# A rotation's eight matrix squarings: by four pairs at once, and half of the pairs summed on TensorE and taken out by ScalarE

## The chip, the cores and the metric

The kernel runs on one core of a Trainium2 chip. The time is device microseconds of one execution. Engines are called PE (TensorE), DVE (VectorE), ACT (ScalarE), POOL (GpSimd) and SP (the engine that issues DMAs here). The kernel before takes 2093.96 us, the median of three runs from 2091.3 to 2096.46 us.

## The reference, cut to what matters

Sixteen samples x[s] of 256 x 288 are first rotated, and then go through three layers of attention and a feed-forward part. The change is in the rotation alone:

```
v = silu(cond) @ W.T + b              # 2016 numbers per sample
A = skew-symmetric 64 x 64 matrix of v
R = expm(A)                           # one rotation per sample
Q = orthonormal basis of P (288 x 64) # by elimination
x = x + x Q (R - I) Q^T               # in effect: x is rotated in the space of P
# then three layers: attention, gelu/feed-forward, modulated by cond
```

## The kernel before

`prepare` does the rotation; it ends about 170 us into the span, and the three layers take the rest. It does two things at the same time.

**The elimination.** DVE orthogonalises P column by column, in nine phases k = 0 to 8 of eight steps i each. A step is a chain of seven small dependent instructions (sign, turn, update of the tile, reciprocal, factors, next column, outer product: L969 to L1015) of 0.15 to 0.23 us. Between two phases PE, DVE and ACT hand over to each other (`change_phase` on PE, `norms`, `whole_t_out`, `both_out` on ACT): DVE writes `whole` (L1022), PE transposes it (L574, chain_a and chain_b), DVE writes `spread`, ACT writes the norms and copies `whole_t` (L462, L463, L467), and PE multiplies by `whole_t` (L593, L595), which starts the next phase.

**The exponential.** A is scaled by 2^-8, its exponential E (less the identity) comes from a power series, and is squared eight times: with E for exp - I, one squaring is 2E + E·E. Since A is skew, the tile `ef` (here with the trace's name skew_ef) holds for each of eight pairs of samples E and its transpose (m = 0 and 1), 128 columns of a pair; the two samples of a pair lie on the lower and upper 64 partitions. A squaring in one round of all samples is 4 fills f: `square(f)` on PE makes the products of two pairs (8 matmuls, 16 records in the trace, because a 4-byte matmul is recorded twice) into half of bank ps_a or ps_b in turn, and `squared(f)` on DVE (L922) computes 2·ef + bank over 256 columns and writes ef. There are 32 fills. The table `places` puts each `squared` behind a step of the elimination on DVE: eight in phase 5, nine each in 6 and 7, six in 8. The table `SQUARES` spreads the matmuls in the same way over PE's program.

**Other work in these phases.** For two samples per phase PE transposes x (`transposed`, L629), ACT copies the transposed pieces out (`transposed_out`, L431, L432), and PE multiplies them (`in_space`, L637). In phases 6 and 8 PE also computes the modulation (`modulation_rows`, L673, L677; ACT copies them, L444, L445; `modulation_columns` on PE, L685; `mods_out` on ACT, L453). In phases 6, 7 and 8 ACT rounds weights of the first layer (`high_weights`, L418), in program order ahead of the norms of the phase.

Every engine runs its program in the order written in its function of `prepare`; nothing is scheduled by a planner. After phase 8, DVE makes `diag`, `inv_beta` and `c_mat`, then `low_weights(0)` (L1090), and then copies `c_t` (L1095) from the matmul at L737; the rotations, the differences and the first layer's q and k follow from c_t.

Of the kernel before, what the change touches and what calls it, by code (L numbers as in the profile page):

```python
# [8 lines left out]
ALU = mybir.AluOpType  # L9
# [50 lines left out]
def prepare(nc, dram, keep, early):  # L60
# [10 lines left out]
    with ExitStack() as ctx:  # L71
# [30 lines left out]
        even = sb("even", [P, NPAIR, R])  # L102
        mod_rows = sb("mod_rows", [P, L, ROW_COLS])
# [73 lines left out]
        s_exp = sem("s_exp")  # L177
        s_square_ps = sem("s_square_ps")
# [48 lines left out]
        FILLS = 4 * SQUARINGS  # L227
        GROUPS = ((0, 5), (5, 10), (10, B))

        SQUARES = {5: range(0, 8), 6: range(8, 17), 7: range(17, 26), 8: range(26, FILLS)}  # L230

# [22 lines left out]

        def pairs_of(f):
            return slice(2 * (f % 4), 2 * (f % 4) + 2)
# [113 lines left out]
        def _(act):  # L370
# [21 lines left out]
            A(gram_norm[TOP, 0:1], unit[TOP, 0:1], ACT.Sqrt)  # L392
            for half in range(2):
                A(twin[:, half, :], unit[TOP, TOP_COLS], ACT.Copy).then_inc(s_twin, 1)
# [43 lines left out]
            def powers_out(n):  # L438
                act.wait_ge(s_product, n + 1)
                A(powers[:, :, n, :], (ps_a, ps_b)[n][:, :].rearrange("p (n c) -> p n c", c=R), ACT.Copy).then_inc(s_power, 1)  # L440

# [41 lines left out]
            for k in range(PHASES):  # L483
# [11 lines left out]
                if k == POWERS_AT:  # L495
                    powers_out(0)
                    powers_out(1)
                for s in INPUTS.get(k, ()):
                    transposed_out(s)
                    if s % 2:  # L500
                        in_space_out(s // 2)
# [3 lines left out]
                if k in (6, LAST):  # L505
                    mod_rows_out(k // LAST)
                    mods_out(k // LAST)
# [50 lines left out]
        def _(pe):  # L558
# [97 lines left out]
            def square(f):  # L656
                bank = (ps_a, ps_b)[f % 2]
                pe.wait_ge(s_exp, 2 + max(f - 1, 0))
                pairs = range(pairs_of(f).start, pairs_of(f).stop)
                for i, n in enumerate(pairs):  # L660
# [31 lines left out]
            for k in range(PHASES):  # L692
# [24 lines left out]
                for i, f in enumerate(SQUARES.get(k, ())):  # L717
                    square(f)
                    if i == 1:
                        transposed(INPUTS[k][0])  # L720
                    if i == 3:
                        transposed(INPUTS[k][1])
                    if i == 5:
                        in_space(INPUTS[k][0] // 2)
                    if k == 6 and i == 6:
                        modulation_rows(0)
                    if k == 6 and i == 8:
                        modulation_columns(0)
                if k == LAST:
                    modulation_rows(1)  # L730
                    modulation_columns(1)
# [3 lines left out]
            pe.wait_ge(s_twin, 2)  # L735
# [5 lines left out]
            pe.wait_ge(s_exp, 2 + FILLS)  # L741
# [94 lines left out]
        def _(dve):  # L836
# [82 lines left out]
            def squared(f):  # L919
                dve.wait_ge(s_square_ps, f + 1)  # L920
                here = ef[:, pairs_of(f), :, :].rearrange("p n m c -> p (n m c)")
                V.scalar_tensor_tensor(out=here, in0=here, scalar=2.0, in1=(ps_a, ps_b)[f % 2][:, 0:256],  # L922
                                       op0=ALU.mult, op1=ALU.add).then_inc(s_exp, 1)
# [20 lines left out]
            DONE = len(places)  # L944
# [1546 lines left out]
```

## Time and profile before

| what | value |
|---|---|
| median of three runs | 2093.96 us |
| the profiled execution's own time | 2095.36 us |
| its span | 2093.7 us |
| PE busy, its weight loads busy | 94%, 84% |
| DVE, ACT, POOL busy | 58%, 54%, 48% |
| mean granted TensorE clock | 0.967 |
| first squaring's matmuls | at 73.24 us |
| c_t (behind the last phase) | at 129.99 us |

The shares are means over the span, and nearly all of the span is the layers. The change lies between 73 and 130 us, so only the timeline of that stretch tells what it does. PE there is shown twice in a timeline: PEld are weight loads, and PE are matmuls, whose ends are modelled. The clock column PEclk is 1.00 for 2.4 GHz and 0.50 for 1.2 GHz.

### The profile page before, as it was taken

The page shows a single profiled execution, that of the slowest core. Times are in us where ns is not written, and L with a number is a line of the kernel's source. Part 1 is how long each engine was busy: PE and PEld are TensorE (multiplying, and loading weights), DVE is VectorE, ACT ScalarE, POOL GpSimd, SP SyncE. Part 2 cuts the span into 40 slices and gives each one's busy share as a digit, 9 for nine tenths or more (in the row PEclk, how much of TensorE's full clock was granted, in tenths as well). Part 3 has the DMA queues.
Part 4 walks back from the last instruction along what each step waited for, and adds up shares of the span by engine and source line. Part 5 has one row for each costly group of instructions (what it writes and reads, how often), then busy time and mean ns, then how long its engine had stood idle before and what let it go on. Part 6 is the DMA issues. An engine that isn't in the chain of part 4 may idle for free. (4 is left out here: it accounts for less than half of the span.)

```text
span 2093.7 us, 49820 instructions
## 1 busy us (share of the span) xinstructions
PE 1977.5 (94%) x16599; PEld 1757.2 (84%) x16599; DVE 1205.1 (58%) x2656; ACT 1120.6 (54%) x1928; POOL 1006.7 (48%) x1037
## 2 busy tenths in 40 slices
PE   5886799999999999899999999998999999999996
PEld 3554589899999998789899998997889998999986
DVE  7874556556465575556565465575565465554641
ACT  5322464655656645555655646555555646556552
POOL 1002455455554554655454454555655554555534
PEclk9787899999999999999999999999999999999998
DMA  7514433333323333433333323333433323333320
GB/s 204 134 61 120 145 101 80 103 90 92 99 80 106 97 84 102 152 100 90 94 87 101 99 80 103 91 92 99 135 86 99 99 79 105 92 91 96 84 81 26
DMA packets 138467, 207.01 MB, mean 99 GB/s; under 512 B 35720, under 2 KB 95718, under 8 KB 137318
## 3 DMA queue, kind: packets, MB, share of 16 engines
q1 hardware_dynamic: 110338, 168.31, 29.2%
q10 hardware_dynamic: 25332, 29.74, 5.2%
q0 software_dynamic: 2704, 7.77, 1.4%
q8 instruction: 53, 0.87, 0.2%
q14 instruction: 40, 0.33, 0.1%
HBM read 99.18 MB, written 20.82 MB: 57 GB/s over the span
## 5 line engine op out<-in xcount | busy, mean ns | idle before, releaser
L2255 DVE TENSOR_REDUCE maxima<-scores 128x4 f32<-128x1024 f32 x384 | 460.9, 1223 | 180.4 <-PE scores L2011 173.4
L1618 POOL TENSOR_TENSOR hidden<-g_full,hidden 128x512 fp32r<-128x512 f32 (+1 forms) x240 | 280.5, 1176 | 356.6 <-ACT hidden L1852 355.4
L1809 ACT ACTIVATE probs<-scores 128x1024 f32<-128x1024 f32 x384 | 383.2, 1027 | 98.7 <-PE pv_ps L2048 58.8
L2073 PE MATMUL mlp_ps<-h_mlp,w_up 128*128 128x256 f32 (+1 forms) x3024 | 404.6, 286 | 5.0 <-POOL h_mlp L1618 3.4
L2073 PEld LDWEIGHTS mlp_ps<-h_mlp,w_up 128*128 128x128 f32 (+1 forms) x3024 | 378.6, 190 | 35.4 <-issue 19.4
L1936 PE MATMUL mlp_ps<-w_down,hidden 128*128 128x288 f32 x2592 | 390.8, 296 | 0.0
L1936 PEld LDWEIGHTS mlp_ps<-w_down,hidden 128*128 128x128 f32 x2592 | 370.0, 189 | 18.6
L2011 PE MATMUL scores<-k_stack,q_stack 108*128 108x512 f32 x768 | 241.9, 407 | 8.9 <-DMA k_stack<-qk 6.8
L2034 PE MATMUL scores<-q_stack,k_stack 110*128 110x256 f32 x1536 | 247.0, 293 | 3.4 <-ACT probs L1809 2.2
L2034 PEld LDWEIGHTS scores<-q_stack,k_stack 110*128 110x128 f32 x1536 | 209.3, 192 | 33.0 <-issue 18.9
L1799 ACT ACTIVATE neg_max<-att_ps 16x256 fp32r<-16x256 f32 x48 | 17.9, 374 | 380.9 <-PE att_ps L2021 380.9
L1686 POOL TENSOR_TENSOR o_full<-o_full,inv_sum 128x512 f32<-128x512 f32 x96 | 139.7, 1475 | 156.1 <-DVE o_att L2267 156.1
L2260 DVE RECIPROCAL inv_few<-sums 128x32 f32<-128x32 f32 x48 | 16.9, 353 | 317.5 <-DMA sums<-sum_scratch 317.5
L1851 ACT ACTIVATE g_full<-mlp_ps 128x512 f32<-128x512 f32 (+1 forms) x240 | 133.4, 556 | 122.5 <-PE mlp_ps L2073 61.3
L1618 POOL TENSOR_TENSOR h_mlp<-h_full,h_mlp 128x512 fp32r<-128x512 f32 x48 | 72.5, 1510 | 260.0 <-DVE h_mlp L2221 259.8
L2048 PE MATMUL pv_ps<-probs,v_sb 128*32 128x256 f32 x3072 | 190.0, 388 | 0.6 <-ACT probs L1809 0.6
L1936 PE MATMUL mlp_ps<-w_out,o_att 128*128 128x288 f32 x1152 | 173.3, 301 | 5.1 <-issue 4.1
L1936 PEld LDWEIGHTS mlp_ps<-w_out,o_att 128*128 128x128 f32 x1152 | 159.7, 192 | 6.9 <-issue 4.5
L2011 PEld LDWEIGHTS scores<-k_stack,q_stack 108*128 108x128 f32 x768 | 129.2, 194 | 21.6 <-DVE maxima L2255 8.8
L2048 PEld LDWEIGHTS pv_ps<-probs,v_sb 128*32 128x32 f32 x3072 | 91.0, 111 | 65.9 <-issue 4.1
L1985 PE MATMUL att_ps<-h_att,w_in 128*126 128x256 f32 (+3 forms) x987 | 134.3, 283 | 1.6 <-DVE qk L2231 0.9
L1852 ACT ACTIVATE hidden<-mlp_ps 128x512 fp32r<-128x512 f32 (+1 forms) x240 | 132.0, 550 | 0.0
(263 smaller groups left out, 2843.4 us busy)
## 6 DMA issues: line engine op xcount, KB each, us to landing
q_stack<-qk SPq DMA_DIRECT2D x144, 180.0 KB
k_stack<-qk SPq DMA_DIRECT2D x282, 90.0 KB
inv_sum<-inv_scratch ACTq DMA_DIRECT2D x192, 128.0 KB, 2.7
k_stack<-qk SPq DMA_DIRECT2D x282, 54.0 KB
x_mid<-out_x SPq DMA_DIRECT2D x48, 288.0 KB, 4.2
out_x<-x_out SPq DMA_DIRECT2D x48, 288.0 KB, 3.1
x_in<-out_x SPq DMA_DIRECT2D x46, 288.0 KB, 3.9
q_stack<-qk SPq DMA_DIRECT2D x144, 72.0 KB
```

The source lines that it names most:

```text
L1618: tt(out, full, high.bitcast(F32), ALU.subtract).then_inc(signal, 1)
L1686: tt(o_full[:, half, :], o_full[:, half, :], inv_sum[:, half, :], ALU.mult).then_inc(s_o_norm, 1)
L1809: evict(probs[:, u % 4, :, :, :], scores[u % 2][:, :, :, :], ACT.Exp, scale=SCALE)\
L1851: evict(g_full[:, n % 2, 0:width], bank[:, 0:width], ACT.Gelu_apprx_tanh).then_inc(s_gelu, 1)
L1852: evict(hidden[0][:, tiles, :].rearrange("p a t -> p (a t)"), bank[:, 0:width], ACT.Gelu_apprx_tanh)\
L1936: last = mm(out, a(left), c(weights[w]), start=start and n == 0, stop=stop and n == total - 1)
L1985: last = mm(qk_bank[n][0:cols.stop - cols.start, (m % 2) * T:(m % 2 + 1) * T], w[:, cols], h, start=count == 0, stop=count == 6)
L2011: last = mm(scores[u % 2][:, qt, :, :], q_stack[r, u, qt * P:(qt + 1) * P], k_stack[r, u, :, :], start=True, stop=True)
L2034: last = mm(scores[u % 2][:, par, kt, :], k_stack[r, u, par, kt * P:(kt + 1) * P], q_stack[r, u, :], start=True, stop=True)
L2048: last = mm(pv_ps[32 * i:32 * i + 32, (g % 2) * T:(g % 2 + 1) * T], v_sb[:, kt, 4 * g + i, :], probs[:, u % 4, i % 2, kt, :], start=kt == ...
L2073: last = mm(up_bank[n % 2][:, (m % 2) * T:(m % 2 + 1) * T], w[:, m * P:(m + 1) * P], h, start=count == 0, stop=count == 6)
L2255: nc.vector.tensor_reduce(out=maxima[:, :, :, u], in_=scores[u % 2][:, :, :, :], axis=AX.X, op=ALU.max).then_inc(s_max, 1)
```

## The change

Round r of the squarings now works on four pairs at once. Pairs 0 to 3 stay with DVE: PE writes all of their products into the whole of ps_a (16 matmuls), and DVE adds 2·ef over 512 columns. For pairs 4 to 7, PE also multiplies ef by a new constant `twice` (two times the identity) and accumulates this and the product in ps_b (32 matmuls); ACT then copies the 512 columns out to ef. Each of phases 5 to 8 holds two rounds: DVE's part stands behind steps 2 and 6 (5 in the last phase), PE's at the start of the phase and behind `in_space`, and ACT's ahead of `transposed_out` and ahead of `mods_out` and `high_weights`. `modulation_rows` now stands ahead of the second round on PE, `modulation_columns` behind it.

```
-        FILLS = 4 * SQUARINGS
-        SQUARES = {5: range(0, 8), 6: range(8, 17), 7: range(17, 26), 8: range(26, FILLS)}
+        SQUARES = {5: (0, 1), 6: (2, 3), 7: (4, 5), 8: (6, 7)}
...
+            for h, cols in ((TOP, TOP_COLS), (GRAM, GRAM_COLS)):
+                A(twice[h, :], unit[h, cols], ACT.Copy, scale=2.0).then_inc(s_twin, 1)
...
+            def squared(r):                                   # on ACT
+                act.wait_ge(s_square_ps, 2 * r + 2)
+                A(ef[:, 4:NPAIR, :, :].rearrange("p n m c -> p (n m c)"), ps_b[:, :], ACT.Copy).then_inc(s_exp_others, 1)
...
+                if k in SQUARES:                              # ACT, ahead of transposed_out
+                    squared(SQUARES[k][0])
...
+                if k in SQUARES:                              # ACT, behind mod_rows_out
+                    squared(SQUARES[k][1])
+                if k in (6, LAST):
                     mods_out(k // LAST)
                 if k in (6, 7, 8):
                     high_weights(k - 6)
...
-            def square(f):
-                bank = (ps_a, ps_b)[f % 2]
-                pe.wait_ge(s_exp, 2 + max(f - 1, 0))
+            def square(r):
+                pe.wait_ge(s_exp, 2 + r)
+                for n in range(4):
                     for m in range(2):
-                        at = (2 * i + m) * R
-                        last = halves(bank[:, at:at + R], ef[:, n, 1 - m, :], ef[:, n, m, :])
+                        at = (2 * n + m) * R
+                        last = halves(ps_a[:, at:at + R], ef[:, n, 1 - m, :], ef[:, n, m, :])
+                last.then_inc(s_square_ps, 1)
+
+            def square_others(r):
+                if r == 0:
+                    pe.wait_ge(s_twin, 2)
+                pe.wait_ge(s_exp_others, r)
+                for n in range(4):
+                    for m in range(2):
+                        at = (2 * n + m) * R
+                        for first in (True, False):
+                            for h in (TOP, GRAM):
+                                last = mm(ps_b[h, at:at + R], twice[h, :] if first else ef[h, 4 + n, 1 - m, :], ef[h, 4 + n, m, :],
+                                          start=first, stop=not first, tile_position=(h.start, h.start))
                 last.then_inc(s_square_ps, 1)
...
+                if k in SQUARES:                              # PE
+                    square(SQUARES[k][0])
+                    square_others(SQUARES[k][0])
+                    for n in INPUTS[k]:
+                        transposed(n)
+                    in_space(INPUTS[k][0] // 2)
+                    if k in (6, LAST):
+                        modulation_rows(k // LAST)
+                    square(SQUARES[k][1])
+                    square_others(SQUARES[k][1])
+                    if k in (6, LAST):
+                        modulation_columns(k // LAST)
...
-            def squared(f):
-                dve.wait_ge(s_square_ps, f + 1)
-                here = ef[:, pairs_of(f), :, :].rearrange("p n m c -> p (n m c)")
+            def squared(r):                                   # on DVE
+                dve.wait_ge(s_square_ps, 2 * r + 1)
+                here = ef[:, 0:4, :, :].rearrange("p n m c -> p (n m c)")
...
-            places = [(5, i) for i in (*range(1, 7), GAP_A, GAP_B)]
-            places += [(k, i) for k in (6, 7) for i in (*range(7), GAP_A, GAP_B)]
-            places += [(8, i) for i in range(6)]
+            places = [(k, i) for k in (5, 6, 7, 8) for i in (2, 6 if k < LAST else 5)]
```

PE in phase 6 before, from in_space (xt_ps) over modulation_rows (ada_ps from w_ada_0) to the first transpose of the change of phase (chain_a); ps_a and ps_b from skew_ef are the squarings:

```order
L637 MATMUL xt_ps<-x_t,p_nat 64x256 x6
L569 MATMUL ps_a<-skew_ef 64x64 x8
L673 MATMUL ada_ps<-w_ada,silu_c 16x352 x4
L677 MATMUL ada_ps<-w_ada,silu_c 16x144 x4
...
L569 MATMUL ps_b<-skew_ef 64x64 x8
L569 MATMUL ps_a<-skew_ef 64x64 x8
L685 MATMUL ada_ps<-ident,mod_rows 128x128 x2
L685 MATMUL ada_ps<-ident,mod_rows 96x128
L574 MATMUL chain_a<-ident,whole 64x64 x2
```

The same place of the changed kernel:

```order
L647 MATMUL xt_ps<-x_t,p_nat 64x256 x6
L696 MATMUL ada_ps<-w_ada_0,silu_c 16x352 x4
L700 MATMUL ada_ps<-w_ada_0,silu_c 16x144 x4
...
L579 MATMUL ps_a<-skew_ef 64x64 x16
L685 MATMUL ps_b<-skew_ef,twice 64x64 x2
L685 MATMUL ps_b<-skew_ef 64x64 x2
...
L708 MATMUL ada_ps<-ident,mod_rows 128x128 x2
L708 MATMUL ada_ps<-ident,mod_rows 96x128
L584 MATMUL chain_a<-ident,whole 64x64 x2
```

Between modulation_rows and modulation_columns there were 16 matmuls in two fills, and there are now 48 in one round (the last two rows on ps_b alternate, two matmuls each, eight times).

ACT in phase 7 before, from in_space's copy (w_rot_x) over the weights' rounding (w_in0) to the norms and whole_t:

```order
L436 ACTIVATE w_rot_x<-xt_ps 128x256
L418 ACTIVATE w_in0<-staging 128x5x36 x2
L418 ACTIVATE w_in0<-staging 128x2x36
L418 ACTIVATE w_in0<-staging 128x3x36
L418 ACTIVATE w_in0<-staging 128x2x18
L418 ACTIVATE w_in0<-staging 128x288
L462 ACTIVATE gram_norm<-turn 64x8
L463 ACTIVATE norm<-turn 64x8
L467 ACTIVATE whole_t<-chain_b 128x72
```

And in the changed kernel:

```order
L436 ACTIVATE w_rot_x<-xt_ps 128x256
L445 ACTIVATE skew_ef<-ps_b 128x512
L418 ACTIVATE w_in0<-staging 128x5x36 x2
L418 ACTIVATE w_in0<-staging 128x2x36
L418 ACTIVATE w_in0<-staging 128x3x36
L418 ACTIVATE w_in0<-staging 128x2x18
L418 ACTIVATE w_in0<-staging 128x288
L467 ACTIVATE gram_norm<-turn 64x8
L468 ACTIVATE norm<-turn 64x8
L472 ACTIVATE whole_t<-chain_b 128x72
```

The copy of the second round (skew_ef from ps_b) now stands ahead of the rounding and of the norms.

## Rows read from the trace of the kernel before

**Rows 1.** Windows; columns: stretch, length, busy of PE, PEld, DVE, ACT, POOL, clock, DMA, GB/s.

```profile
58.50:79.00 20.50, 18.15 (x150) 12.58 (x146) 16.90 (x92) 6.58 (x23) 0.17 (x1) 0.50 0.92 208
102.90:106.30 3.40, 3.35 (x41) 3.19 (x42) 3.05 (x17) 0.94 (x6) 0.00 (x0) 0.50 1.01 224
```

**Rows 2.** Timeline; columns: start, length, engine, line, operation, [idle before]. DVE's fills of 256 and 512 columns.

```profile
65.51 0.69 DVE L910 SCALAR_TENSOR_TENSOR odd<-ada_ps,a_pos 128x512 f32<-128x512 f32 x1
...
76.23 0.41 DVE L922 SCALAR_TENSOR_TENSOR skew_ef<-skew_ef,ps_a 128x256 f32<-128x256 f32 x1
76.56 0.15 DVE L969 TENSOR_SCALAR sign<-current 128x1 f32<-128x1 f32 x1
...
78.06 0.15 DVE L969 TENSOR_SCALAR sign<-current 128x1 f32<-128x1 f32 x1
```

**Rows 3.** Timeline: bursts of 64x64 matmuls at the low and the high clock.

```profile
73.24 0.98 PEld L569 LDWEIGHTS ps_a<-skew_ef 64*64 64x64 f32 x14
...
74.31 0.98 PEld L569 LDWEIGHTS ps_b<-skew_ef 64*64 64x64 f32 x14
...
131.00 1.01 PEld L569 LDWEIGHTS ps_a<-c_twice,skew_ef 64*64 64x64 f32 x32 [0.38 <-DVE c_twice L1097]
...
132.20 0.69 DVE L1102 COPY w_rot_x<-ps_a 128x512 f32<-128x512 f32 x1
```

**Rows 4.** Timeline, phase 6: PE and ACT in turn on the transposed input.

```profile
87.52 0.86 PE L629 MATMUL xt_ps<-ident,w_rot_x 128*96 128x128 f32 x6
...
88.42 0.59 ACT L431 ACTIVATE x_t<-xt_ps 96x512 f32<-96x512 f32 x1 [0.48 <-PE xt_ps L629]
...
88.91 0.37 ACT L432 ACTIVATE x_t<-xt_ps 96x256 f32<-96x256 f32 x1
...
90.98 0.24 PEld L629 LDWEIGHTS xt_ps<-ident,w_rot_x 128*96 128x96 f32 x2
...
92.00 0.37 ACT L432 ACTIVATE x_t<-xt_ps 96x256 f32<-96x256 f32 x1
...
93.61 1.52 PE L637 MATMUL xt_ps<-x_t,p_nat 96*64 96x256 f32 x12
...
95.05 0.54 PEld L569 LDWEIGHTS ps_a<-skew_ef 64*64 64x64 f32 x16 [0.39 <-issue]
```

**Rows 5.** Timeline: the end of phase 6, and the first squaring of phase 7.

```profile
95.66 0.13 PEld L673 LDWEIGHTS ada_ps<-w_ada,silu_c 96*16 96x16 f32 x8
...
98.30 0.54 PEld L569 LDWEIGHTS ps_b<-skew_ef 64*64 64x64 f32 x16 [0.24 <-issue]
...
99.38 0.29 PEld L685 LDWEIGHTS ada_ps<-ident,mod_rows 128*128 128x128 f32 x3
...
100.91 1.41 ACT L418 ACTIVATE w_in<-staging 128x180 fp32r<-128x180 f32 x6
102.34 0.21 ACT L462 ACTIVATE gram_norm<-turn 64x8 f32<-64x8 f32 x1
...
102.95 0.18 PEld L593 LDWEIGHTS chain_b<-both,whole_t 64*64 64x64 f32 x1 [2.14 <-ACT whole_t L467]
...
103.12 0.98 PEld L569 LDWEIGHTS ps_b<-skew_ef 64*64 64x64 f32 x14
```

**Rows 6.** Timeline: the first squarings of phases 6 and 8.

```profile
86.33 0.59 PEld L569 LDWEIGHTS ps_a<-skew_ef 64*64 64x64 f32 x15
...
116.38 0.89 PEld L569 LDWEIGHTS ps_a<-skew_ef 64*64 64x64 f32 x15
```

**Rows 7.** Timeline: behind the last step of phase 8.

```profile
127.56 0.15 DVE L969 TENSOR_SCALAR sign<-current 64x1 f32<-64x1 f32 x1
...
128.41 1.39 DVE L1090 TENSOR_TENSOR w_in<-staging,w_in 128x180 fp32r<-128x180 f32 x6
...
129.99 0.28 DVE L1095 COPY c_t<-chain_a 64x128 f32<-64x128 f32 x1 [0.19 <-PE chain_a L737]
```

**Rows 8.** Timeline: SP issues the first layer's q.

```profile
166.61 14.47 SPq L1368 DMA_DIRECT2D q_stack<-qk  x12
```

More of the change, by code:

```diff
@@ L102, in prepare @@
         even = sb("even", [P, NPAIR, R])
+        twice = sb("twice", [P, R])
         mod_rows = sb("mod_rows", [P, L, ROW_COLS])
@@ L177, in prepare @@
         s_exp = sem("s_exp")
+        s_exp_others = sem("s_exp_others")
         s_square_ps = sem("s_square_ps")
@@ L253, in x_banks @@
             return (ada_ps if s % 2 else xt_ps)[:, s % 2, :], xt_ps[:, 1, 0:T]
-        def pairs_of(f):
-            return slice(2 * (f % 4), 2 * (f % 4) + 2)
         def halves_of(k):
@@ L654, in high_powers @@
                         last.then_inc(s_product, 1)
-            def square(f):
-                bank = (ps_a, ps_b)[f % 2]
-                pe.wait_ge(s_exp, 2 + max(f - 1, 0))
-                pairs = range(pairs_of(f).start, pairs_of(f).stop)
-                for i, n in enumerate(pairs):
-                    for m in range(2):
-                        at = (2 * i + m) * R
-                        last = halves(bank[:, at:at + R], ef[:, n, 1 - m, :], ef[:, n, m, :])
+            def square(r):
+                pe.wait_ge(s_exp, 2 + r)
+                for n in range(4):
+                    for m in range(2):
+                        at = (2 * n + m) * R
[12 more added lines that the diff above has]
+                                          start=first, stop=not first, tile_position=(h.start, h.start))
                 last.then_inc(s_square_ps, 1)
@@ L716, in _ @@
                             in_space(s // 2)
[L717 to L731, printed above, removed]
+                if k in SQUARES:
[10 more added lines that the diff above has]
+                        modulation_columns(k // LAST)
                 if k < LAST:
                     change_phase(k)
-            pe.wait_ge(s_twin, 2)
+            pe.wait_ge(s_twin, 4)
             pe.wait_ge(s_c_mat, 1)
@@ L740, in _ @@
             pe.wait_ge(s_basis, 16)
-            pe.wait_ge(s_exp, 2 + FILLS)
+            pe.wait_ge(s_exp, 2 + SQUARINGS)
+            pe.wait_ge(s_exp_others, SQUARINGS)
             mm(ps_b[:, 0:C], c_t[:, :, :], p_t[:, :], start=True, stop=True).then_inc(s_u_ps, 1)
@@ L917, in exponential @@
                                        op0=ALU.mult, op1=(ALU.add, ALU.subtract)[m]).then_inc(s_exp, 1)
-            def squared(f):
-                dve.wait_ge(s_square_ps, f + 1)
-                here = ef[:, pairs_of(f), :, :].rearrange("p n m c -> p (n m c)")
-                V.scalar_tensor_tensor(out=here, in0=here, scalar=2.0, in1=(ps_a, ps_b)[f % 2][:, 0:256],
-                                       op0=ALU.mult, op1=ALU.add).then_inc(s_exp, 1)
+            def squared(r):
+                dve.wait_ge(s_square_ps, 2 * r + 1)
+                here = ef[:, 0:4, :, :].rearrange("p n m c -> p (n m c)")
+                V.scalar_tensor_tensor(out=here, in0=here, scalar=2.0, in1=ps_a[:, :], op0=ALU.mult, op1=ALU.add).then_inc(s_exp, 1)
             def inverse_norms():
@@ L940, in _ @@
             between.update({(8, 0): (inverse_norms,), (8, 1): (inverse_norms_diagonal,)})
-            places = [(5, i) for i in (*range(1, 7), GAP_A, GAP_B)]
-            places += [(k, i) for k in (6, 7) for i in (*range(7), GAP_A, GAP_B)]
-            places += [(8, i) for i in range(6)]
-            DONE = len(places)
+            places = [(k, i) for k in (5, 6, 7, 8) for i in (2, 6 if k < LAST else 5)]
             def fill(k, i):
```

## The prediction

> **What bounds the kernel now.** I read the page's busy shares first: PE leads with 94%, but that is the layers. The change lies between 73 and 130 us, so I went on to the windows and then the timeline of that stretch, engine by engine. The reader is to see two things there. In phases 5, 7 and most of 8, DVE's chain of elimination steps is the pace: its instructions follow each other without a gap, and a fill lies in it [rows 2]. At the ends of phases 6 and 8 it is not DVE: the first matmuls of phase 7 wait 2.14 us for ACT's whole_t, which stands behind the rounding of weights [rows 5], and in phase 8 c_t waits at the end for PE [rows 7]. What the change takes from DVE it gives to PE and ACT, so I work out each phase anew as a chain over all three and compare it with the phase's length before. The phases begin, by the first squaring's weight load, at 73.24, 86.33, 103.12 and 116.38 us, and c_t comes at 129.99 [rows 3, 5 to 7]: lengths 13.09, 16.79, 13.26 and 13.61 us.
>
> **What DVE is spared.** A fill of 256 columns lasts 0.41 us, but the next sign starts 0.33 behind its start; a step with one takes 78.06 - 76.56 = 1.50, so about 1.17 without. 512 columns with one operand in PSUM last 0.69 [rows 2], 0.28 more, so 0.61 in the chain. Removed: 32 x 0.33 = 10.6 us. Added: 8 x 0.61 = 4.9. If DVE alone were the pace, that would be 5.7 us less.
>
> **What PE gets.** 32 fills of 8 matmuls were 256; now 8 rounds of 16 + 32 are 384. In the trace's records (two per matmul) a round is 96. At 2.4 GHz 32 records start within 1.01 us and DVE can read the result 1.20 after the first [rows 3], so a round takes 3 x 1.01 = 3.03 us with the gaps between its parts, and DVE's part is there at 1.20. At 1.2 GHz two bursts of 16 matmuls together, 32 records, take 74.31 + 0.98 - 73.24 = 2.05, so a round 6.15. Accumulating pairs of this kind are not in the trace; I take them at the price of the plain ones. Lower bound: 16 records start within 0.54 us [rows 4], 0.027 each with the last one's own 0.13 taken off; upper bound: 15 within 0.59 right after a change of phase [rows 6], 0.033 each. With two rounds of 96 in a phase that is from -0.4 to +0.5 us per phase against the 3.03. ACT's copy of 512 columns: 0.59, the next instruction 0.49 behind its start [rows 4]; between 0.49 and DVE's 0.69, I take 0.49.
>
> **The chain of a phase.** PE's program is now: round, transposed (first sample), transposed (second), in_space, in phases 6 and 8 modulation_rows, second round, in phases 6 and 8 modulation_columns, change of phase. Before, the DVE chain hid the whole exchange with ACT between the fills; now it stands in one row with both rounds. From rows 4: the transposes start and ACT is done with the first sample 88.91 + 0.37 - 87.52 = 1.76 us later; the last transposes of the second start then, and ACT is done 92.37 - 90.98 = 1.39 later; in_space takes 95.05 - 93.61 = 1.44 until PE goes on. With 0.05 for each hand-over that is 4.70 us. A clean round ahead of it (3.03) puts the second round at 7.75, DVE's second fill at 8.95. Eliminating alone, DVE would want it at about 0.3 + 1.3 + 5 x 1.17 + 0.61 + 1.1 = 9.1, so it hardly waits there in phases without modulation, at the high clock.
>
> Phase 5. The clock is at 1.2 GHz until 79 us [rows 1], so the first round ends at about 79.15, not 76.3. Then 4.70: second round at 83.85; its 96 records end at 86.9; ACT's copy starts at 87.1 and passes ACT on at 87.6. Behind it stand the norms and whole_t: from L462's start to L593's 0.61, and to the first squaring 0.17 more [rows 5]. Phase 6 starts at 88.35 and not 86.33: +2.0 us. The new ACT copy is the instruction that delays the norms, and PE waits for them.
>
> Phase 6. Round 3.03, exchange 4.70, modulation_rows 98.30 - 95.66 = 2.64 [rows 5], second round at 10.4, its end at 13.4. modulation_columns at 13.45; from there to the rounding of weights 100.91 - 99.38 = 1.53, the rounding 1.43, norms to the next phase 0.78: 17.2 against 16.79, +0.4. DVE waits here for its second fill until 11.6 (it would be ready at 9.1), but then runs 0.61 + 1.0 to `whole` at 13.2, so it isn't what ends last.
>
> Phase 7. Before, the clock was at 1.2 GHz from 102.90 to 106.30 [rows 1], right behind the 2 us that PE sat idle for ACT. That wait stays, so I expect the low stretch again, now over a round of 96 records and not two of 16: 3.4 us at half speed are 53 records, the other 43 take 1.36, so the round takes 4.75. Exchange: second round at 9.45, end at 12.5. ACT's copy 0.15 + 0.49, and only then the rounding of weights, which before had only in_space's copy ahead of it: 1.43, and 0.78. Phase length 15.3 against 13.26: +2.05. At the high clock throughout it would be 13.6: +0.35.
>
> Phase 8. Round, exchange and modulation_rows as in phase 6: second round at 10.4, DVE's fill at 11.6. DVE wants it at about 8.6, and three more dependent pieces stand behind it: 0.61, one step of 1.1, 127.56 to 128.41 = 0.85 to low_weights, and 1.39 for that ahead of c_t [rows 7]. c_t at 15.55 against 13.61: +1.95. Before this phase PE now idles for ACT as well; with a low clock over its round it is +1.7 more. I take the middle, +2.8.
>
> Sum: 2.0 + 0.4 + 2.05 + 2.8 = 7.3 us. Behind c_t everything up to the first layer follows from it: rotations, differences, q and k, and then the q that SP sends from 166.61 on [rows 8]. I count the delay as passed on in full. The two small ACT instructions that make `twice` (0.2 us each) stand near 7 us, ahead of constants that nobody waits for yet: nothing. The profiled execution had 2095.36 us, 1.4 above the median; applied to the median of 2093.96 the sum gives 2101.3 us.
>
> By a page of the Trainium skill ("TensorE: Matmul & The Clock Gate", "Part 1: The HAM clock gate") TensorE is throttled by default and its own activity releases the clock. By that rule the change, which makes PE busier in just these phases, would speak for itself: see the first rival. The trace agrees in that the clock fell behind the idle stretch of phase 6 [rows 1, 5].
> The page "PSUM — Partial Sum Buffer", "Engine vs sequencer instructions", says in the Trainium skill that ScalarE's queue is strict first in, first out. It speaks against the change: the rounding and the norms cannot overtake the new copy. The row in which L593 waits 2.14 us for whole_t agrees [rows 5].
>
> **The rivals.**
> *The busier PE keeps its clock.* In phases 7 and 8 the rounds run at 2.4 GHz: 2.0 + 0.4 + 0.35 + 1.95 = 4.7 us, 2098.7. For it: PE has half again as many squaring matmuls. Against it: PE still idles about 2 us at the ends of 6 and 7 behind ACT, and that is what preceded the low stretch before.
> *DVE is the pace and all else is hidden.* Then the change gives the 5.7 us, 2088.3 us, just inside 0.3%. It decides from the point where the second round is ready before DVE asks, at 9.1 us into the phase, and where ACT's copy ends before the norms. For it: DVE's gapless chain. Against it: modulation_rows alone puts the second round of phases 6 and 8 behind DVE, and ACT's copy comes 3.0 us behind the second round's start, when DVE has nearly finished the phase.
> *It gets worse than that.* More of the exchange falls into low-clock stretches, since PE now works in one burst and then idles through the exchange (about 1.3 us of 4.7), and the accumulating pairs cost the upper bound: 7.3 + one stretch of 1.7 + 4 x 0.5 + the rest of phase 8's 0.8 = 11.8, 2105.8 us.
> *The delay is absorbed* by SP's and the DMA queues' 14 us behind 166.61 [rows 8], if these wait for bandwidth that was used by something not delayed: 0 to 3 us, 2095.5.
>
> **How the numbers follow.** 0.3% is 6.3 us, about what a measurement of this kernel can tell from no change. The forecast has 0.55 (its own range 4.7 to 9.7 us, about 2098.7 to 2103.7), the kept clock 0.2, DVE as the pace 0.07, worse 0.12, absorbed 0.06. Slower by over 0.3%: three quarters of the forecast and all of the worse case and a bit, 0.55. Faster: half of DVE's rival and less, 0.03. Within: 0.42. Range: 2095.5 to 2106.
>
> **What would show it.** In the profile after: PE's first squaring of phase 6 at 88.3 and not 86.3; ACT's copy of 512 columns starting after 87 us, with the norms right behind; DVE idle for 2 to 3 us ahead of its second fill in phases 6 and 8, and not in 7; the weights' rounding of phase 7 behind the second copy; c_t near 137 us. The clock column at the starts of phases 7 and 8 tells the forecast from the first rival. It is wrong if c_t comes ahead of 130 us, if DVE has no idle time in phase 8, or if a round of 96 records takes well under 3 us.

## The result, and the profile after

The changed kernel takes 2100.61 us (median of 8 runs, 2094.05 to 2104.41) against 2093.78 us for the kernel before (8 runs, 2089.16 to 2098.02). The ratio is 1.0033, with a 95% interval from 1.0017 to 1.0050: 6.8 us slower. The profiled execution has 2103.66 us and a span of 2101.7 us. All ratios here are of executions in one state; a single one of the twelve of run r3, at 2126.03 us and a mean granted clock of 0.898, is left aside as slow.

The phases can be followed by PE's first load behind whole_t (L593 before, L603 after), which starts each phase; lines from here on are those of the kernel named. c_t is DVE's copy that ends the stretch. The forecast's lengths count from the first squaring's load, 0.1 us behind that.

| | phase 5 | phase 6 | phase 7 | phase 8 to c_t | c_t behind the start of phase 5 |
|---|---|---|---|---|---|
| before | 13.15 | 16.73 | 13.31 | 13.73 | 56.9 |
| changed | 14.20 | 20.20 | 15.13 | 15.51 | 65.0 |
| forecast | 15.1 | 17.2 | 15.3 | 16.4 | 64.0 |

c_t comes at 137.98 us, 7.99 later than before [rows 7]. Behind it the delay stays: SP issues the first q at 175.70, 9.1 later than in [rows 8], the first load of x_mid is issued 8.7 us later and the last 7.8 (210.9 and 2036.3 against 202.2 and 2028.5).

First PE's weight loads in phases 5 and 6 of the changed kernel, from the timeline (start, length, engine, line, operation, [idle before and its releaser]):

```profile
73.11 1.83 PEld L579 LDWEIGHTS ps_a<-skew_ef 64*64 64x64 f32 x30
...
78.19 0.61 PEld L639 LDWEIGHTS xt_ps<-ident,w_rot_x 128*96 128x96 f32 x6
...
82.83 1.01 PEld L579 LDWEIGHTS ps_a<-skew_ef 64*64 64x64 f32 x32 [0.39 <-issue]
...
85.51 0.20 PEld L685 LDWEIGHTS ps_b<-skew_ef 64*64 64x64 f32 x4
...
87.14 0.13 PEld L603 LDWEIGHTS chain_b<-both,whole_t 64*64 64x64 f32 x1 [0.30 <-ACT whole_t L472]
...
95.20 0.15 PEld L696 LDWEIGHTS ada_ps<-w_ada,silu_c 96*16 96x16 f32 x8 [0.64 <-issue]
...
100.29 1.52 PEld L579 LDWEIGHTS ps_a<-skew_ef 64*64 64x64 f32 x32 [0.46 <-issue]
...
107.34 0.13 PEld L603 LDWEIGHTS chain_b<-both,whole_t 64*64 64x64 f32 x1 [2.17 <-ACT whole_t L472]
```

Compare with [rows 3 to 5]. The exchange of the transposed input is 82.83 - 78.19 = 4.64 us, as worked out from the rows of before (4.70). The second round of phase 5 takes 85.51 + 0.20 - 82.83 = 2.88 us at the high clock (3.03 had been counted). modulation_rows, though, take 100.29 - 95.20 = 5.1 us, where [rows 5] have 2.64.

ACT in the same kernel: its second copies (L445), what stands behind them, and the norms (L467):

```profile
85.90 0.60 ACT L445 ACTIVATE skew_ef<-ps_b 128x512 f32<-128x512 f32 x1 [2.56 <-PE ps_b L685]
86.52 0.21 ACT L467 ACTIVATE gram_norm<-turn 64x8 f32<-64x8 f32 x1
...
103.86 0.60 ACT L445 ACTIVATE skew_ef<-ps_b 128x512 f32<-128x512 f32 x1 [2.79 <-PE ps_b L685]
...
105.30 1.41 ACT L418 ACTIVATE w_in<-staging 128x180 fp32r<-128x180 f32 x6
106.73 0.21 ACT L467 ACTIVATE gram_norm<-turn 64x8 f32<-64x8 f32 x1
...
119.97 0.60 ACT L445 ACTIVATE skew_ef<-ps_b 128x512 f32<-128x512 f32 x1 [2.56 <-PE ps_b L685]
120.46 1.37 ACT L418 ACTIVATE w_in<-staging 128x180 fp32r<-128x180 f32 x6
121.86 0.21 ACT L467 ACTIVATE gram_norm<-turn 64x8 f32<-64x8 f32 x1
```

In phases 5 and 7 ACT's copy ends right ahead of the norms or of the rounding that they stand behind; in phase 6 the modulation's columns (`mods_out`, 104.36 to 105.44) come between the copy and the rounding. In phase 7 the rounding (120.46) was in ACT's idle time before and is in the row now. A copy passes ACT on after 0.49 to 0.62 us.

DVE's second fill in phases 5 to 8, and c_t:

```profile
84.03 0.69 DVE L944 SCALAR_TENSOR_TENSOR skew_ef<-skew_ef,ps_a 128x512 f32<-128x512 f32 x1 [1.45 <-PE ps_a L579]
...
102.00 0.69 DVE L944 SCALAR_TENSOR_TENSOR skew_ef<-skew_ef,ps_a 128x512 f32<-128x512 f32 x1 [5.46 <-PE ps_a L579]
...
118.11 0.69 DVE L944 SCALAR_TENSOR_TENSOR skew_ef<-skew_ef,ps_a 128x512 f32<-128x512 f32 x1 [1.37 <-PE ps_a L579]
...
134.11 0.69 DVE L944 SCALAR_TENSOR_TENSOR skew_ef<-skew_ef,ps_a 128x512 f32<-128x512 f32 x1 [3.05 <-PE ps_a L579]
...
137.98 0.28 DVE L1113 COPY c_t<-chain_a 64x128 f32<-64x128 f32 x1
```

DVE is no longer the pace in any of the four phases; ahead of its four second fills it waits 11.3 us in all for PE's products. The wait in phase 6 is twice what was forecast (2 to 3 us), and the part beyond the forecast goes with the clock: in the second profile below, where the clock is up, it is 2.23 us. One window of that stretch (busy us of PE, PEld, DVE, ACT, POOL; then clock, DMA, GB/s), first in this profile, and then in a second profile of the same kernel (r1 below). What made the clock fall in one and not in the other stays open.

```profile
94.80:101.30 6.50, 6.50 (x70) 2.86 (x68) 1.59 (x10) 1.03 (x3) 0.00 (x0) 0.50 0.00 0
```

```profile
94.80:101.30 6.50, 6.29 (x157) 4.78 (x145) 2.88 (x15) 1.95 (x11) 0.00 (x0) 1.00 0.59 132
```

### The profile page after: what moved, and what is told of

Same layout as the page of the kernel before. It is cut to its first block and busy times, and to the rows that moved or that the text cites. A ratio compares the mean times of both kernels' runs of the same rounds, so it can differ in the third digit from the quotient of the medians.

```text
span 2101.7 us, 50320 instructions
## 1 busy us (share of the span) xinstructions
PE 1976.9 (94%) x16855; PEld 1762.0 (84%) x16855; DVE 1199.0 (57%) x2632; ACT 1126.6 (54%) x1938; POOL 1007.0 (48%) x1037
```

## The experiments

All kernels build on the changed one unless said otherwise. The two columns of the table that decide are the ratio to the kernel before, of many runs, and c_t behind the start of phase 5 in one profile each. The clock falls at other places in each execution, so a phase in which it was low for over 1 us is marked *.

| | ratio, 95% interval | phase 5 | 6 | 7 | 8 | c_t behind start |
|---|---|---|---|---|---|---|
| before | 1 | 13.15 | 16.73 | 13.31* | 13.73* | 56.9 |
| changed | 1.0033 (1.0017 to 1.0050) | 14.20 | 20.20* | 15.13* | 15.51 | 65.0 |
| r1, changed again | one run | 13.32 | 16.98 | 14.91* | 15.50 | 60.7 |
| r2, changed again | one run | 14.25 | 20.20* | 14.98* | 16.90* | 66.3 |
| e1 rows last | 1.0005 (0.9992 to 1.0019) | 14.05 | 17.61 | 14.89* | 14.98 | 61.5 |
| e2 weights first | 1.0017 (1.0003 to 1.0031) | 14.62* | 15.70 | 16.53* | 15.51 | 62.4 |
| e3 all on DVE | 0.9987 (0.9974 to 0.9999) | 13.08 | 16.64* | 12.76* | 16.09* | 58.6 |
| e4 no doubled | 0.9987 (0.9974 to 1.0001) | 12.42 | 15.11 | 12.87* | 16.08* | 56.5 |
| e5 interleaved | 0.9959 (0.9947 to 0.9971) | 12.43 | 13.76 | 14.84* | 13.95* | 55.0 |
| r3, e5 again | 0.9965 (0.9951 to 0.9980) | 12.48 | 13.76 | 14.51* | 13.30* | 54.1 |
| e6 before, weights first | 0.9994 (0.9982 to 1.0006) | 13.14 | 15.48 | 13.31 | 14.17* | 56.1 |
| e7 filler | 1.0037 (1.0022 to 1.0052) | 14.82 | 17.51 | 16.73* | 17.61* | 66.7 |
| e8 interleaved, all on DVE | 0.9966 (0.9952 to 0.9980) | 13.09 | 12.89 | 12.69 | 13.72* | 52.4 |
| e9 before reordered | 0.9984 (0.9971 to 0.9997) | 13.15 | 14.04 | 13.08 | 13.43* | 53.7 |

(The start of phase 5 is at the low clock in all of them; the * of e2 there is a second low stretch.)

### The same kernel twice more: r1, r2

> The changed kernel once more, for another profile. If the low clock over modulation_rows in phase 6 (94.8 to 101.3 us in the first profile) belongs to this order, it shows again at that place and phase 6 takes about 20 us; if it depends on how the execution happens to lie against the clock, it is elsewhere or gone and phase 6 takes 17 to 17.5 us.

> The same again: a third profile of the changed kernel, with the same two readings as the second.

No edit. 2099.98 and 2100.77 us. The low clock over modulation_rows shows in two of three profiles of the changed kernel. Phase 6 is 20.20, 16.98 and 20.20 us: with the clock up it is the forecast's 17.2. These rows are from r1, and stand against those of the first profile above:

```profile
94.34 0.13 PEld L696 LDWEIGHTS ada_ps<-w_ada,silu_c 96*16 96x16 f32 x8 [0.39 <-issue]
...
96.97 1.01 PEld L579 LDWEIGHTS ps_a<-skew_ef 64*64 64x64 f32 x32 [0.24 <-issue]
...
99.92 0.29 PEld L708 LDWEIGHTS ada_ps<-ident,mod_rows 128*128 128x128 f32 x3
...
103.52 0.18 PEld L603 LDWEIGHTS chain_b<-both,whole_t 64*64 64x64 f32 x1 [2.17 <-ACT whole_t L472]
```

modulation_rows take 2.63 us here in place of 5.1, and the 3.2 us between the two lengths of phase 6 go with the low stretch. c_t is 3.8 us later than before in r1 and 8.1 in the first profile. So about half of what one profile says of c_t can be the clock's luck, and single profiles are to be compared phase by phase, with the clock beside them.

### What the added matmuls cost: e4

This kernel leaves out the summand 2E for pairs 4 to 7, and so doesn't compute the rotation; only its time is used.

```
-                        for first in (True, False):
-                            for h in (TOP, GRAM):
-                                last = mm(ps_b[h, at:at + R], twice[h, :] if first else ef[h, 4 + n, 1 - m, :], ef[h, 4 + n, m, :],
-                                          start=first, stop=not first, tile_position=(h.start, h.start))
+                        last = halves(ps_b[:, at:at + R], ef[:, 4 + n, 1 - m, :], ef[:, 4 + n, m, :])
```

> The changed kernel without the matmuls of the doubled matrix: for pairs 4 to 7 the sum 2E is left out and only E*E is made and copied, so PE does 64 and not 96 records per round. Theory (every PE microsecond of a round is in the row but for the last): 7 rounds shorter by 0.93 us each, one or two of them at half clock by 1.9, so c_t 7 to 9 us earlier, at 129 to 131, near the kernel before. Rival (order is all: where a round stands matters and not how long it is): c_t less than 3 us earlier.

c_t 8.5 us earlier than in the changed kernel's first profile (56.5 against 65.0), 2090.86 us, ratio 0.9987. Without the clock's part: phase 6 is 15.11 against 16.98 in r1, and phase 7, with a low stretch in both, 12.87 against 14.91. Two rounds per phase shorter by 32 records each should give 2 x 0.93 = 1.9, and give 1.87 and 2.04. In phases 6 and 7 PE's time in both rounds is in the row, microsecond for microsecond. For phase 8 the fair partner is r2, with a low stretch at the start of both: 16.08 against 16.90, 0.8 us. Only the first of its two rounds lies ahead of DVE's second fill there, and c_t comes 3.87 us behind that fill in e4, r2 and the changed kernel alike.

### What ACT's order costs: e2

```
+                if k in (6, 7, 8):
+                    high_weights(k - 6)
                 if k in (6, LAST):
                     mod_rows_out(k // LAST)
                 if k in SQUARES:
                     squared(SQUARES[k][1])
                 if k in (6, LAST):
                     mods_out(k // LAST)
-                if k in (6, 7, 8):
-                    high_weights(k - 6)
```

> The changed kernel, with ACT's rounding of weights (high_weights, 1.4 us) ahead of mod_rows_out and of the second copy, in time in which ACT waits. Theory (the norms stand in a row behind the second copy and the rounding): phases 6 and 7 are 1.4 us shorter each, c_t at about 135.1, the time 2.9 us below the changed kernel. Rival (the granted clock alone explains the added time): c_t stays at 138 but for what the clock does.

Phase 6: 15.70 against 16.98 in r1, 1.3 us shorter, close to the 1.4 expected. In phase 7 the norms do follow the copy at once:

```profile
115.84 1.38 ACT L418 ACTIVATE w_in<-staging 128x180 fp32r<-128x180 f32 x6
118.51 0.60 ACT L445 ACTIVATE skew_ef<-ps_b 128x512 f32<-128x512 f32 x1 [1.29 <-PE ps_b L685]
119.13 0.21 ACT L467 ACTIVATE gram_norm<-turn 64x8 f32<-64x8 f32 x1
```

but the phase was no shorter, since something else came in: 3.26 us in which PE stood still within a round, for nothing that the profile shows, and a low clock behind it. Less these 3.26 us it would have 13.3 (14.91 in r1), which fits the 1.4 us but doesn't show them. By the two ratios the time is 3.3 us below the changed kernel's, where 2.9 were expected, but the intervals overlap (1.0003 to 1.0031 against 1.0017 to 1.0050), so the gain in time isn't shown; what is shown is phase 6.

```profile
108.64 0.13 PEld L685 LDWEIGHTS ps_b<-skew_ef,twice 64*64 64x64 f32 x1 [3.26 <-issue]
```

### Whether DVE's idle time is the cost: e1

```
                     in_space(INPUTS[k][0] // 2)
-                    if k in (6, LAST):
-                        modulation_rows(k // LAST)
                     square(SQUARES[k][1])
                     square_others(SQUARES[k][1])
                     if k in (6, LAST):
+                        modulation_rows(k // LAST)
                         modulation_columns(k // LAST)
```

> The changed kernel, with modulation_rows moved behind the second round on PE (and ACT's second copy ahead of mod_rows_out). DVE's idle time ahead of its second fill in phases 6 and 8 (5.5 and 3.1 us in the changed kernel) should mostly go. Theory (PE's program in a row, with ACT's copies and norms behind it, is the length of a phase; DVE's idle time lies beside it): PE's sum of work per phase is unchanged and modulation_columns now wait 0.6 us for ACT's rows, so c_t comes within about 1 us of the changed kernel's 137.98 us, and the time is the changed kernel's, about 2100 to 2102. Rival (DVE's idle time is the cost): c_t 5 to 8 us earlier, 130 to 133, and the time near that of the kernel before.

The clean comparison is phase 8, at the high clock here and in the changed kernel: DVE's wait for the second fill goes from 3.05 to 0.41 us, but the phase from 15.51 to 14.98 only, because c_t now waits for PE:

```profile
127.79 0.69 DVE L942 SCALAR_TENSOR_TENSOR skew_ef<-skew_ef,ps_a 128x512 f32<-128x512 f32 x1 [0.41 <-PE ps_a L578]
...
133.77 0.28 DVE L1111 COPY c_t<-chain_a 64x128 f32<-64x128 f32 x1 [2.03 <-PE chain_a L755]
```

Phase 6 is 17.61 against r1's 16.98, 0.6 longer, as worked out. So DVE's idle time lies beside PE's row, and taking it away gives 0.5 us or costs 0.6. The time, however, was 2094.43 us, ratio 1.0005, where no change against the changed kernel's 1.0033 was expected. The expectation missed here. c_t in the one profile (61.5) is 3.5 us below the first profile of the changed kernel and 0.8 above r1's, so it isn't the place. The traces show where the time went: behind c_t, where the instructions are the same. Each line of this table gives the time from c_t to SP's first load of x_mid, the mean granted clock in it, and SP's loads of x_mid from the first to the last, over the layers:

| | c_t to first x_mid | clock | first to last x_mid |
|---|---|---|---|
| before | 72.2 | 0.71 | 1826.3 |
| changed, r1, r2 | 72.9, 71.9, 71.8 | 0.69, 0.71, 0.71 | 1825.4, 1826.9, 1823.2 |
| e1 | 67.7 | 0.78 | 1823.4 |
| e2, e4 | 69.7, 69.0 | 0.75, 0.76 | 1822.4, 1823.7 |
| e3, e8 | 70.4, 71.5 | 0.74, 0.71 | 1825.9, 1824.3 |
| e5, r3 | 67.8, 69.9 | 0.80, 0.76 | 1823.7, 1821.7 |
| e6, e9 | 67.8, 66.3 | 0.78, 0.79 | 1832.2, 1826.3 |
| e7 | 71.7 | 0.74 | 1820.6 |

On the whole the stretch behind c_t is the shorter, the less of it lies at the low clock, and e1's is 4 to 5 us shorter than the changed kernel's. More than one execution says so: the mean granted clock of e1's ten runs is 0.973, and that of the changed kernel's eight 0.969 (0.969 and 0.967 in r1 and r2). Why this order meets fewer low stretches stays open. A ratio of these kernels thus holds two things, c_t and what the clock does behind it.

### The clock, filled up: e7

```
+            def filler(r, count):
+                pe.wait_ge(s_exp_others, r + 1)
+                for n in range(count):
+                    at = n % 8 * R
+                    halves(ps_b[:, at:at + R], ef[:, 4, 0, :], ef[:, 4, 1, :])
...
                     if c == 2:
+                        if s in (9, 11, 13, 15):
+                            filler(s - 9, 6)
                         pe.wait_ge(s_xt, 2 * s)
...
+                    filler(SQUARES[k][0], 10)
                     in_space(INPUTS[k][0] // 2)
```

The second piece stands in transposed: the filler writes ps_b ahead of each sample's third column block, and again ahead of in_space.

> The changed kernel, with matmuls whose result is overwritten (into ps_b) where PE waits for ACT between the transposes and ahead of in_space, 12 and 20 matmuls a phase. Theory of the clock (the low stretch over modulation_rows in phase 6 follows from PE's idle time in the exchange): the clock column stays at 1.00 from about 80 us to the end of phase 6, modulation_rows take 2.6 us and not 5.1, and phase 6 is 16.8 to 17.5 us and not 20.2; c_t at about 135. Rival (the low stretch has another cause, or the fillers cost what they bring): phase 6 stays near 20 us or every phase grows by 0.5 us.

The clock stayed up from 78 to 104.7 us and phase 6 took 17.51 us, but r1 has the clock up without a filler and takes 16.98, so this run proves nothing for the filler, and the rival by which it costs 0.5 us a phase fits as well. c_t came at 139.5 us, where 135 was expected: phases 7 and 8 grew to 16.73 and 17.61 us (low stretches over both, and 1.3 us of PE standing still), and the ratio is 1.0037. Filling PE's waits doesn't pay here.

### Half of the change, alone: e3

```
-                if k in SQUARES:
-                    squared(SQUARES[k][0])
...
+            def square(r, other=0):
...
+                        last = halves(bank[:, at:at + R], ef[:, 4 * other + n, 1 - m, :], ef[:, 4 * other + n, m, :])
...
             def square_others(r):
+                square(r, 1)
...
+            def squared(f):
+                dve.wait_ge(s_square_ps, f + 1)
+                here = ef[:, 4 * (f % 2):4 * (f % 2) + 4, :, :].rearrange("p n m c -> p (n m c)")
...
-            places = [(k, i) for k in (5, 6, 7, 8) for i in (2, 6 if k < LAST else 5)]
+            places = [(k, i) for k in (5, 6, 7, 8) for i in ((2, 3, 6, GAP_A) if k < LAST else (2, 3, 5, 6))]
```

Both halves of the pairs get the same 16 matmuls, into ps_a and ps_b, DVE adds 512 columns in 16 fills, and both copies on ACT are gone.

> Only the first half of the change: four pairs at once, rounds at the same places on PE, but no doubled matrix and no copies on ACT; DVE sums all, in 16 fills of 512 columns behind steps 2, 3, 6 and the gap (2, 3, 5, 6 in the last phase). Theory: a round is 64 records (2.0 us), the norms have nothing new ahead of them, so phase 5 is about as before (13.1 us), phase 6 about 15.5, phase 7 about 13, phase 8 about 15 because its second round stands behind modulation_rows: c_t between 128 and 131, the time that of the kernel before within 3 us. Rival (the order with both rounds and the exchange in one row costs the time, not the doubled matrix and the copies): c_t 134 or later.

c_t at 131.2 (58.6 behind the start, with a low stretch over phase 6 and one over phase 8), the time 2091.38 us, ratio 0.9987. Four pairs at once, with the same order of rounds and all sums on DVE, is no slower than before, and 0.46% faster than the changed kernel by the two ratios. What made the change slow are the parts that e3 leaves out: the doubled matrix on PE, and the copies on ACT.

### The same work in another order: e5, and again as r3

```
                     square(SQUARES[k][0])
-                    square_others(SQUARES[k][0])
-                    for n in INPUTS[k]:
-                        transposed(n)
-                    in_space(INPUTS[k][0] // 2)
-                    if k in (6, LAST):
-                        modulation_rows(k // LAST)
+                    transposed(INPUTS[k][0])
+                    square_others(SQUARES[k][0])
+                    transposed(INPUTS[k][1])
                     square(SQUARES[k][1])
+                    in_space(INPUTS[k][0] // 2)
                     square_others(SQUARES[k][1])
                     if k in (6, LAST):
-                        modulation_columns(k // LAST)
+                        modulation_rows(k // LAST)
                 if k < LAST:
                     change_phase(k)
+                if k == 6:
+                    modulation_columns(0)
...
             mm(chain_b[:, 256:256 + R], twin[:, :, :], c_mat[:, :], start=True, stop=True).then_inc(s_c_ps, 1)
+            modulation_columns(1)
```

On ACT the first copy stands between the two samples' transposed_out, high_weights ahead of mod_rows_out, and the second copy and mods_out behind the hand-over.

> All of the changed kernel's work in another order: on PE first round for DVE, transposes, first round for ACT, transposes, second round for DVE, in_space, second round for ACT, modulation_rows, change of phase, modulation_columns; on ACT the rounding of weights first, the norms and the hand-over, and then the second copy and mods_out. Theory (order and waits, not PE's added work, can be hidden): phase 5 as before (13.0), phase 6 about 13.3, phase 7 about 12.2, phase 8 about 12.7: c_t at about 124 to 125, 5 to 6 us below the kernel before and 13 below the changed one; the time about 2088. Rival (384 matmuls in place of 256 don't fit beside the elimination): c_t not below 129.

> The interleaved kernel e5 once more. Its first profile had a low clock from 109 to 116 us, across the end of phase 7 and the start of phase 8, and lengths 12.43, 13.76, 14.84 and 13.97 us. If that stretch belongs to the order (PE idle behind the second round while DVE finishes the phase), it shows again and phase 7 is above 14 us; if it depends on how the execution lies against the clock, phase 7 is 12.2 to 13 us and c_t 52.5 to 53.5 us behind the start of phase 5, no later than in e8. The ratio to before again between 0.994 and 0.998.

2085.37 and 2084.76 us, ratios 0.9959 and 0.9965: the fastest of all, 15 us below the changed kernel with the same instructions. Now PE's rounds fill its waits for ACT, and ACT's copy stands behind the norms. c_t was expected at 124 to 125 and came at 127.2 and 126.7. Most of what is missing is in phase 7, in both profiles (14.84 and 14.51 against 12.2 expected), the rest in phase 8 (13.95 and 13.30 against 12.7): again PE stood still within a round, and the clock fell behind it:

```profile
110.93 0.29 PEld L685 LDWEIGHTS ps_b<-skew_ef,twice 64*64 64x64 f32 x4 [3.25 <-issue]
```

```profile
111.34 0.19 PEld L685 LDWEIGHTS ps_b<-skew_ef,twice 64*64 64x64 f32 x4 [3.17 <-issue]
```

This answers r3's question: the standstill belongs to this order, since it came again behind the same instruction, the 40th of the round's 64 records into ps_b. Of the 9 us against the kernel before, 2 to 3 lie ahead of c_t; in the profiles another 4.4 and 2.3 us lie between c_t and the first x_mid (67.8 and 69.9 us against 72.2), where the same instructions meet less of the low clock (0.80 and 0.76 against 0.71), and 2.6 and 4.6 over the layers, whose lengths differ by as much between profiles of one kernel (1823.2 to 1826.9 in the changed one).

### The order without the squarings: e6 and e9

e6 is the kernel before with high_weights ahead of mod_rows_out. e9 also has

```
                 if k in (6, LAST):
                     mod_rows_out(k // LAST)
-                    mods_out(k // LAST)
...
                     reset(k)
+                if k in (6, LAST):
+                    mods_out(k // LAST)
...
-                    if k == 6 and i == 8:
-                        modulation_columns(0)
                 if k == LAST:
                     modulation_rows(1)
-                    modulation_columns(1)
                 if k < LAST:
                     change_phase(k)
+                if k == 6:
+                    modulation_columns(0)
...
             mm(chain_b[:, 256:256 + R], twin[:, :, :], c_mat[:, :], start=True, stop=True).then_inc(s_c_ps, 1)
+            modulation_columns(1)
```

That is, ACT's mods_out goes behind the hand-over, and PE's modulation_columns behind the change of phase (6) or behind c_mat's two products (8).

> The kernel before, with only ACT's rounding of weights moved ahead of mod_rows_out in phases 6 and 8. Theory: in phase 6 the norms stood behind mods_out and the rounding, so phase 6 is 1.4 us shorter and c_t at about 128.6; with less idle time on PE at the end of phase 6 the low clock at the start of phase 7 may go as well, which is hidden there by DVE. The time 1 to 2 us below before. Rival: the weights aren't there in time and ACT waits for them, c_t as before or later.

> The kernel before with its 32 fills, and only the order of the other work as in e5: on ACT the rounding of weights first and mods_out behind the hand-over, on PE modulation_columns behind the change of phase. Theory: phase 6 loses the 1.4 us of the rounding and the 1.1 us of mods_out and modulation_columns' 0.5, so it takes 13.5 to 14.5 us in place of 16.7, the other phases as before: c_t 53.5 to 55 us behind the start of phase 5 (before: 56.9), so this explains more than half of e5's gain over before, and the four pairs at once little. Rival (e5's gain is the squarings'): c_t 56 us or more behind the start.

e6: phase 6 is 15.48 (-1.25), c_t at 128.8, as expected; in time 0.9994, not to be told from no change. Phase 7 takes 13.31 us as before, now without a low stretch: in the kernel before, that stretch was hidden behind DVE. e9: phase 6 is 14.04, c_t 53.7 behind the start (-3.2), ratio 0.9984 (0.9971 to 0.9997). Both within their expectations: the kernel before lost 3 us to the order of ACT's and PE's other work, which has nothing to do with squarings. In c_t e9 is as good as e5 (its phase 7 has no standstill); in time e5 is 5 us better, and c_t doesn't explain that. The profile of e9 can't either: its execution has 2085.55 us, 5.4 below the median of its twelve, with the clock at 0.79 behind c_t.

### What is left of the doubled matrix: e8

e8 is e5's order with e3's content (no doubled matrix, no copies on ACT, 16 fills on DVE).

> The interleaved order of e5 with e3's content: four pairs at once, but DVE sums all 16 fills of 512 columns, and there is neither a doubled matrix nor a copy on ACT. Theory (in the interleaved order DVE is the pace, so taking sums from DVE pays): against e5 DVE has 8 more fills of 0.61 us in its chain, less those in the gap, so c_t 2 to 4 us later than e5's (which was 55.0 us behind the start of phase 5; here 57 to 59). Rival (PE's 96 records are the pace in e5 too): c_t at the same place or earlier than in e5.

The theory missed: c_t is 52.4 us behind the start, 1.7 to 2.6 us earlier than in e5, not 2 to 4 later. e5's two profiles have the standstill of 3.2 us in phase 7, though, so the phases without it decide. In phase 6 e8 takes 12.89 and e5 13.76 us, and at its end DVE waits for PE in e5 and doesn't in e8:

```profile
97.35 0.23 DVE L1058 TENSOR_TENSOR spread<-chain_a,both 128x64 f32<-128x64 f32 x1 [1.57 <-PE chain_a L584]
```

So in the interleaved order, too, PE's row with its 96 records a round is the pace in a phase with modulation, and taking sums from DVE buys nothing there. In phase 5 it does (12.43 against 13.09). The times (0.9966 against 0.9959 and 0.9965) can't be told apart.

## Why the prediction was right

The measured median, 2100.6 us, is 0.7 us from the forecast 2101.3 us, and its ratio clear of 1. The mechanism was right as well; the sum comes out so close because the misses of its terms cancel. Step by step:

- *DVE is not the pace any more; each phase is a row over PE and ACT.* Right. e4 shows PE's part (1.9 us per phase for 64 records in phases 6 and 7), e2 ACT's (1.3 us in phase 6), e1 that DVE's idle time is beside it (0.5 us in phase 8), by the lengths of the phases and not by the time. The signs named for DVE were not all right: it was to wait in phases 6 and 8 "and not in 7", and waited 1.37 us there and 1.45 in phase 5. The prediction's own sums put the second fill at 10.65 and 11.8 us into these phases, behind the 9.1 at which DVE would want it, so the sign contradicted them.
- *Prices.* The exchange 4.64 (4.70), a high-clock round 2.88 (3.03), ACT's copy 0.49 to 0.62 (0.49), DVE's 512 columns 0.61 to the next sign (0.61): read off the rows of before, all hold. The accumulating matmuls cost what plain ones do. The bounds given for them were summed wrongly: 0.027 and 0.033 us for each of 192 records are 5.2 and 6.3 us against 6.06, so about -0.8 to +0.3 us per phase and not -0.4 to +0.5; the rival "worse" then has 10.9 and not 11.8 us.
- *Phase 5: +2.0, measured +1.05.* The size was off, mostly because the clock rose at 77.5 and not at 79 us: the first round ended at 78.1 and not 79.15, and ACT's copy started at 85.9 and not 87.1. In the other profiles the phase has +0.17 and +1.10.
- *Phase 6: +0.4, measured +3.47.* The mechanism was right (r1: +0.25), the clock was not foreseen: it fell over modulation_rows in two of three profiles, worth 3.2 us; why it fell is open. PE's waits in the exchange had been counted as time, but not as a danger for the clock, which the worse rival alone named.
- *Phase 7: +2.05, measured +1.82* (1.60 and 1.67 in r1 and r2), with the low stretch over the round that was expected. The rival by which the busier PE keeps its clock fell here: 0.50 over the round in each of the three profiles. In phase 8 the clock did stay up in two of them.
- *Phase 8: +2.8 as a middle of 1.95 and 3.6; measured +1.78, 1.77 and 3.17.* Both ends were seen.
- *Passed on in full.* In the first profile, 8.0 us at c_t and 7.8 at the last x_mid. In r1 and r2 c_t is 3.9 and 8.5 us later than before and the last x_mid 4.2 and 5.0, with 3 us between the layers' lengths. The rival of a delay absorbed behind 166 us fell: the first x_mid is 8.7, 3.6 and 8.1 us later.
- *DVE as the pace with all else hidden* fell in the changed kernel, but it was the useful rival: e5 comes near it in phase 5 by moving PE's and ACT's work into the waits.

Part of the closeness is luck: in the first profile phase 5's and 8's terms were too large by 2 us together, phase 6's too small by 3. With the clock of r1 the same kernel has c_t 3.8 us later than before, and not 7.3; the mean of the three profiles is 7.1.

## What to carry to other kernels

Before work is moved off an engine that looks like the pace, write down the row of every other engine that it is moved to, with its waits: here 5.7 us were taken from DVE, and what PE and ACT got made the kernel 6.8 us slower. The same instructions in an order in which each wait is filled by independent work, and with copies behind whatever the next stage waits for, made the kernel 15 us faster than the changed one and 7 to 9 faster than before, part of it by a higher clock behind the stretch. Where one profile's phase is at another clock than the next one's, take a second profile before explaining the difference.

## What the runs showed of the hardware that was not expected

PE can stand still for microseconds within a burst of matmuls that wait for nothing: 3.26 us in e2, 3.25 and 3.17 in e5 and its repeat, 1.30 in e7, and in no profile of the kernels before and changed. All four lie between 105 and 111.4 us, during or just behind the load of the third w_ada (2.2 MB, DMA busy share 0.7 to 1.5 from about 98 to 108 us). In e5 and its repeat PE stopped behind the very same instruction.

That the engine's own instructions come by DMA and were late is an explanation that the traces support. They hold packets of 16 KB on a queue of kind instruction, one every 4 to 11 us in most of the stretch. Around the load they are 13 to 17 us apart in the changed kernel and in these four runs, and the packet behind this gap lies at the standstill:

| | PE stands still | packet of 16 KB | PE goes on behind its end |
|---|---|---|---|
| e2 | 105.38 to 108.64 | 105.93 to 107.19 | 1.45 |
| e5 | 107.68 to 110.93 | 108.33 to 109.64 | 1.29 |
| r3 | 108.17 to 111.34 | 108.75 to 110.07 | 1.27 |
| e7 | 108.78 to 110.08 | 107.21 to 108.44 | 1.64 |

It isn't proved: no run took the load away, and nothing in the trace names the engine that a packet is for. In the changed kernel the packet is as late (107.86 to 109.21), and no standstill comes with it.
